# A graph attention layer with an MLP on one core: edges prepared on GpSimd, other places in the load queue, and a shorter last tile

## The reference

```python
xn = layernorm(x)                       # x: 1250 x 512, 20000 edges (src, dst)
q, k, v = xn@Wq + bq, xn@Wk + bk, xn@Wv + bv          # 4 heads of 512
alpha = sum(q[dst] * k[src]) / sqrt(512)              # one per edge and head
attn  = softmax of alpha over the edges of one dst
x_attn = segment_sum(attn * v[src], dst) + xn@Wskip + bskip
h = x_attn@Wlin + blin + x_attn[:, :512]
x = x + (gamma * (h - mean) / sqrt(var + 1e-5) + beta)
# second part, on z = layernorm(x): four groups of 16 columns are decoded to
# numbers, three MLPs (and, or, xor; 160 wide) run on rows 0 and 1, and of each
# only output column 64 is needed: relu(f@w1 + b1) @ w2[:, 64] + b2[64]
# the MLP is chosen by flags z[1:4]; its rounded output, clipped to 0..15, adds
# 2.0 to one of 16 columns of z (columns 80..95 and 96..111)
x = x + result
```

## Time and profile before

| | us |
|---|---|
| median of 3 runs | 1005.67 |
| lowest and highest of the runs | 1003.58, 1234.95 |
| the profiled execution's own time | 1004.65 |
| span of its instructions | 1002.5 |
| TensorE busy in the span | 984.4 |
| VectorE, ScalarE, GpSimd busy | 579.2, 335.0, 107.7 |

### The profile page before, as it was taken

The page is one execution under the profiler, slowest core; times in us unless marked ns, Lnnn a source line. Parts: engine busy times, 40 slices in busy tenths (PEclk is TensorE's granted clock), DMA queues, the critical chain, the costliest instruction groups (busy, mean ns, idle before and its releaser), DMA issues.

```text
span 1002.5 us, 13135 instructions
## 1 busy us (share of the span) xinstructions
PE 984.4 (98%) x4841; PEld 804.8 (80%) x4841; DVE 579.2 (58%) x1225; ACT 335.0 (33%) x531; POOL 107.7 (11%) x232
## 2 busy tenths in 40 slices
PE   9999999999999999999999999999999999999994
PEld 6667777688888888888888888888888888888883
DVE  6899996452445446226454542354464325788786
ACT  4446554102233223114222321233232213435342
POOL 2121101000000000000000000000000000345465
PEclk9999999999999999999999999999999999999997
DMA  9856554400152344005323420161334103443421
GB/s 327 286 210 210 218 192 189 168 2 1 53 189 68 91 122 146 28 1 157 111 79 105 159 83 1 27 215 53 105 80 163 52 1 83 154 121 105 143 83 40
DMA packets 43561, 115.84 MB, mean 116 GB/s; under 512 B 5472, under 2 KB 26044, under 8 KB 40172
## 3 DMA queue, kind: packets, MB, share of 16 engines
q1 hardware_dynamic: 38892, 98.21, 31.5%
q0 software_dynamic: 4608, 16.78, 4.3%
HBM read 70.07 MB, written 44.90 MB: 115 GB/s over the span
## 4 chain that ended last, share of the span: by engine, by line
PE 94%; DVE 2%; DMA 2%; ACT 1%; issue 1%; SPq 0%; DVEq 0%
PE ps_o L1533 10%; PE ps_o L1534 9%; PE ps_o L1535 9%; PE ps_s L1534 9%; PE ps_r L1533 9%; PE ps_s L1535 9%; PE ps_s L1533 9%; PE ps_r L1535 9%; PE ps_r L1534 9%; PE ps_t L1533 2%; PE ps_t L1535 2%; PE ps_t L1534 2%; DMA stage<-in_Wk 1%; PE ps_s L1612 1%; PE ps_s L1652 1%; DMA early<-in_Wlin 1%
## 5 line engine op out<-in xcount | busy, mean ns | idle before, releaser
L1534 PE MATMUL ps_s<-xT_lo,tT 128*128 128x512 f32 (+1 forms) x480 | 168.7, 351 | 0.0
L1535 PE MATMUL ps_s<-xT_hi,tT 128*128 128x512 f32 (+1 forms) x480 | 168.4, 351 | 0.0
L1533 PE MATMUL ps_s<-xT_hi,tT 128*128 128x512 f32 (+1 forms) x480 | 168.1, 350 | 0.0
L1533 PE MATMUL ps_o<-y,pT 128*128 128x512 f32 x380 | 148.6, 391 | 0.0
L1534 PE MATMUL ps_o<-y,pT 128*128 128x512 f32 x380 | 148.0, 389 | 0.0
L1535 PE MATMUL ps_o<-y,pT 128*128 128x512 f32 x380 | 148.0, 389 | 0.0
L897 ACT ACTIVATE prob<-prob,nbias 128x1250 f32<-128x1250 f32 x40 | 53.7, 1342 | 269.5 <-DVE nbias L1296 269.5
L1290 DVE CUSTOM_DVE_ANT_0 prob<-ps_s,maskb 128x1250 f32<-128x1250 f32 x40 | 58.2, 1456 | 128.9 <-issue 128.9
L1534 PEld LDWEIGHTS ps_s<-xT_lo,tT 128*128 128x128 f32 x480 | 90.7, 189 | 14.1
L1533 PEld LDWEIGHTS ps_s<-xT_hi,tT 128*128 128x128 f32 x480 | 90.5, 189 | 14.0
L1535 PEld LDWEIGHTS ps_s<-xT_hi,tT 128*128 128x128 f32 x480 | 90.8, 189 | 12.5
(11 more groups left out here) (293 smaller groups left out, 1763.0 us busy)
## 6 DMA issues: line engine op xcount, KB each, us to landing
regrouped<-prob SPq DMA_DIRECT2D x156, 160.0 KB, 2.8
whole<-regrouped SPq DMA_DIRECT2D x39, 640.0 KB, 3.9
products<-prod_parts POOLq DMA_DIRECT2D x32, 512.0 KB, 3.9
gbuf<-products SPq DMA_DIRECT2D x4, 2048.0 KB, 8.2
mbuf<-products SPq DMA_DIRECT2D x4, 2048.0 KB, 9.0
stage<-in_Wskip SPq DMA_DIRECT2D x4, 1024.0 KB, 6.0
stage<-in_Wq SPq DMA_DIRECT2D x3, 1024.0 KB, 5.5
stage<-in_Wk SPq DMA_DIRECT2D x3, 1024.0 KB, 5.9
```

Source lines behind the costliest of these rows:

```text
L1533: nc.tensor.matmul(out_, a[0], b[0], start=start, stop=False)
L1534: nc.tensor.matmul(out_, a[0], b[1], start=False, stop=False)
L1535: return nc.tensor.matmul(out_, a[1], b[0], start=False, stop=stop)
```

## The change

- `edge_places` moves from VectorE to GpSimd, where it becomes seven instructions ahead of all product stores. VectorE waits on `edges_ready` where it made them. The edges' four DMAs are issued ahead of operand 2.
- The six later tiles of x are issued behind operand 6, without the waits on stored products, and have a semaphore of their own (`x_more_in`), which VectorE waits for at tile 4.
- The first half of operand 2 is subtracted ahead of the save of block (0, 0), the second half behind it as before.
- `HID` goes from 160 to 162: the second bias of each MLP is the weight of one more hidden unit whose value is always 1. GpSimd's two bias instructions (L693, L694) and the bias DMA go.
- At the end `residual(NT - 1)` runs between the low columns and the decoding of tile NT-2, and the result columns of tile NT-2 are stored by ScalarE's queue.

```diff
-HID = 160
+HID = 162
@@ sync
-            for n in (3, 2):
-                sp.dma_start(early[n - 2][:], weights[n][0]).then_inc(early_in[n - 2], 16)
+            sp.dma_start(early[1][:], weights[3][0]).then_inc(early_in[1], 16)
             for i, ends in enumerate((src, dst)):
                 for a, w in EDGE_ROWS:
                     sp.dma_start(edge_i[a:a + w, i, :], ends[a:a + w, :]).then_inc(edges_in, 16)
+            sp.dma_start(early[0][:], weights[2][0]).then_inc(early_in[0], 16)
...
-            for i in range(KC - 1):
-                sp.wait_ge(prod_out[i], 16)
-            sp.dma_start(acc[:, X_ASIDE:NT - 1, :], x_tiles[:, X_ASIDE:NT - 1, :]).then_inc(x_in, 16)
-            sp.wait_ge(pads_ready, 1)
-            sp.dma_start(acc[0:LAST_ROWS, NT - 1, :], x[full:N, :]).then_inc(x_in, 16)
             for n in load_order():
                 sp.wait_ge(split_ready[n % 2], n // 2 - 1)
                 sp.dma_start(stage[n % 2][:], weights[n % 5][n // 5]).then_inc(stage_in[n % 2], 16)
+                if n == 6:
+                    sp.dma_start(acc[:, X_ASIDE:NT - 1, :], x_tiles[:, X_ASIDE:NT - 1, :]).then_inc(x_more_in, 16)
+                    sp.wait_ge(pads_ready, 1)
+                    sp.dma_start(acc[0:LAST_ROWS, NT - 1, :], x[full:N, :]).then_inc(x_more_in, 16)
...
-            for t in (NT - 1, NT - 2):
-                store_result(t)
+            sp.wait_ge(o_ready, NT - 1)
+            sp.dma_start(out[full:N, result_cols], acc[0:LAST_ROWS, NT - 1, result_cols]).then_inc(out_done, 16)
@@ gpsimd
+            def edge_places():
+                pool.wait_ge(edges_in, 32 * len(EDGE_ROWS))
+                link(nc.gpsimd.tensor_copy(edge_f[0:ER], edge_i[0:ER]))
+                source, place = edge_f[0:ER, 0, :], at_plane[0:ER, :]
+                link(nc.gpsimd.tensor_scalar(place, source, -float(NP // 2), 1.0 / NP, ALU.add, ALU.mult))
+                link(nc.gpsimd.tensor_scalar(place, place, ROUND, None, ALU.add))
+                link(nc.gpsimd.tensor_scalar(place, place, ROUND, None, ALU.subtract))
+                nc.gpsimd.tensor_scalar(weight_i[0:ER, :], place, DIGIT * 2.0 ** 23, ONE_BITS, ALU.mult, ALU.add)
+                link(nc.gpsimd.tensor_scalar(place, place, -float(NP), None, ALU.mult))
+                nc.gpsimd.tensor_tensor(edge_place[0:ER, :], place, source, ALU.add).then_inc(edges_ready, 1)
+            edge_places()
...
-                link(nc.gpsimd.tensor_scalar(sel_, sel_, s_b2[t % 2], 0.0, ALU.add, ALU.max))
-                link(nc.gpsimd.tensor_scalar(sel_, sel_, 15.0, ROUND, ALU.min, ALU.add))
+                link(nc.gpsimd.tensor_scalar(sel_, sel_, 0.0, 15.0, ALU.max, ALU.min))
+                link(nc.gpsimd.tensor_scalar(sel_, sel_, ROUND, None, ALU.add))
...
             z_factors(NT - 2)
             h_factor(NT - 1)
             choice(NT - 2)
-            chosen_bias(NT - 2)
             z_factors(NT - 1)
             choice(NT - 1)
-            chosen_gate(NT - 2)
+            gates(NT - 2)
             gates(NT - 1)
             results(NT - 2)
@@ scalar, at the end
                 feat_copy(NT - 1)
+                act.wait_ge(o_pool, 1)
+                act.dma_start(out[R * BY_POOL:R * BY_POOL + R, result_cols],
+                              acc[0:R, BY_POOL, result_cols]).then_inc(out_done, 16)
@@ vector
-            split_lo_halves(3)
+            split_lo_half(3, 0)
+            split_lo_half(3, 1)
+            split_lo_half(2, 0)
...
                 if p == 0:
                     if i == 0:
-                        split_lo_halves(2)
+                        split_lo_half(2, 1)
                     if i == 2:
-                        edge_places()
+                        dve.wait_ge(edges_ready, 1)
...
-                    dve.wait_ge(x_in, 48)
+                    dve.wait_ge(x_in, 16)
+                if t == X_ASIDE:
+                    dve.wait_ge(x_more_in, 32)
...
                 centre(NT - 1)
+                low_columns(NT - 2)
+                residual(NT - 1)
                 features(NT - 2)
-                residual(NT - 1)
                 choose(NT - 2)
```

More of the change, by code:

```diff
@@ L329, in graph_layer @@
         s_gate = [small[0:R, 78 + i:79 + i] for i in range(2)]
-        s_b2 = [small[0:R, 80 + i:81 + i] for i in range(2)]
         s_act, s_flag = [small[0:R, 82:83], flag_pool[0:R, 0:1]], [small[0:R, 83:86], flag_pool[0:R, 1:4]]
-        s_part = small[0:R, 86:89]
         s_sel, hot = [small[0:R, 90 + 2 * i:92 + 2 * i] for i in range(2)], small[0:R, 96:128]
-        x_in, edges_in, bias_in, tail_in = sem("x_in"), sem("edges_in"), sem("bias_in"), sem("tail_in")
-        blin_in = sem("blin_in")
+        x_in, edges_in, edges_ready, bias_in, tail_in = sem("x_in"), sem("edges_in"), sem("edges_ready"), sem("bias_in"), sem("tail_in")
+        blin_in, x_more_in = sem("blin_in"), sem("x_more_in")
         g_in, m_in, xres_in, out_done = sem("g_in"), sem("m_in"), [sem(f"xres_in{i}") for i in range(3)], sem("out_done")
@@ L559, in store_rest @@
                     sp.dma_start(out[R * t:R * t + rows, a:b], acc[0:rows, t, a:b]).then_inc(out_done, 16)
[L561 to L568, removed]
             def store(t):
@@ L1013, in split_lo, with split_lo_half @@
                                                 ALU.subtract).then_inc(split_ready[odd], 1)
-            def split_lo_halves(n):
-                for half, high in enumerate((half_hi[n - 2], hi_ready[n % 2])):
-                    some = half_cols(half)
-                    dve.wait_ge(high, 1)
-                    ins = nc.vector.tensor_tensor(opnd[n][1][:, :, some], raw(n)[:, :, some],
-                                                  opnd[n][0][:, :, some].bitcast(F32), ALU.subtract)
-                    if half:
-                        ins.then_inc(split_ready[n % 2], 1)
-                    elif n == 2:
-                        ins.then_inc(half_split, 1)
+            def split_lo_half(n, half):
+                some = half_cols(half)
+                dve.wait_ge(hi_ready[n % 2] if half else half_hi[n - 2], 1)
+                ins = nc.vector.tensor_tensor(opnd[n][1][:, :, some], raw(n)[:, :, some],
+                                              opnd[n][0][:, :, some].bitcast(F32), ALU.subtract)
+                if half:
+                    ins.then_inc(split_ready[n % 2], 1)
+                elif n == 2:
+                    ins.then_inc(half_split, 1)
             def onehots(b):
@@ L1422, in chosen_features @@
             def chosen_features(t):
+                low_columns(t)
                 features(t)
@@ L1439, in results @@
                 dve.wait_ge(gate_ready, t + 1)
-                chain(nc.vector.tensor_scalar(sel_, sel_, s_b2[t % 2], 0.0, ALU.add, ALU.max))
-                chain(nc.vector.tensor_scalar(sel_, sel_, 15.0, ROUND, ALU.min, ALU.add))
+                chain(nc.vector.tensor_scalar(sel_, sel_, 0.0, 15.0, ALU.max, ALU.min))
+                chain(nc.vector.tensor_scalar(sel_, sel_, ROUND, None, ALU.add))
                 for r in range(2):
@@ L1894 @@
         for r in range(2):
-            feats[:, o, r:4:2, r, o, :] = np.stack([w1[o][i] for i in (0, 1)])
-            feats[:, o, 4 + 3 * r:7 + 3 * r, r, o, :] = np.stack([w1[o][i] for i in (46, 44, 45)])
-            feats[:, o, 10 + r, r, o, :] = b1[o]
+            feats[:, o, r:4:2, r, o, 0:HID - 2] = np.stack([w1[o][i] for i in (0, 1)])
+            feats[:, o, 4 + 3 * r:7 + 3 * r, r, o, 0:HID - 2] = np.stack([w1[o][i] for i in (46, 44, 45)])
+            feats[:, o, 10 + r, r, o, 0:HID - 2] = b1[o]
+            feats[:, o, 10 + r, r, o, HID - 2] = 1.0
     arrays = {
@@ L1912 @@
         "mlp_w1": feats.reshape(FEAT_ROWS, 2, OPS * HID),
-        "mlp_w2": np.concatenate([g(f"L0_ffn_{o}_w2")[:, 64] for o in ops]),
-        "mlp_b2": np.stack([g(f"L0_ffn_{o}_b2")[64] for o in ops]),
+        "mlp_w2": np.concatenate([np.append(g(f"L0_ffn_{o}_w2")[:, 64], np.array([g(f"L0_ffn_{o}_b2")[64], 0], np.float32)) for o in ops]),
     }
```

36 lines of the change are left out of this document (10 added, 26 removed).

## The result

The changed kernel runs in 998.62 us (median of 6, 997.65 to 1000.16), the kernel before beside it in 1004.23 (median of 6): ratio 0.9946, 95% interval 0.9933 to 0.996. That is 5.6 us faster where 3.4 were forecast; by the 2% measure it is no change. One execution of the kernel before, at 1234.95 us, stands far apart from the others and is left out of the ratio. The profiled execution took 998.57 us, its span 996.4: 6.1 less than before.

A forecast was written before the change was run, and what follows sets the result against it. TensorE, busy 984.4 of 1002.5 us, bounds the kernel; only its idle time can be won. First place 0.7, second 1.6 and tail 1.1 sum to 3.4: 1004.65 - 3.4 = 1001.2 us, range 998.6 to 1004.8.

The forecast's parts named there:

- third and fourth place: Slow edge-counting matmuls of TensorE near 80 and 96 us; the prediction took these stretches for clean and gave no term.
- First place: Edge-counting matmuls from 32.40 us, waiting for VectorE's one-hots: 0.7 us gained of a possible 2.5.
- So the first one-hot comes at 23.2 and not at 21.7: VectorE waits for GpSimd's edges at the first counting place: first one-hot 1.5 us earlier than before, not 3.
- Blocking: GpSimd's edge instructions held up beside VectorE's splits: from 14.2, with 4.0 us of own work, done by 23.2.
- Now it is issued at 23.2; with the median 3.9 us of such a store it lands at 27.1: Store of block (0, 0), behind the edges in GpSimd's queue: VectorE waits 0.8 us, so 1.5 shrink to 0.7.
- Second place: Counting matmuls near 50 us, late because operand 6 landed late; with x tiles behind it, 1.6 us gained.
- Behind 51.6 the view shows no further wait of TensorE until the tail: Claim that after the second counting place TensorE waits nowhere before the tail, so nothing more to win there.
- Tail: Steps after the last aggregation matmul: sooner residual 0.8, split final stores 0.37, less 0.04 for extra columns: 1.1 us.
- The 0.37 for the stores: Two final stores at the end issued from SyncE and ScalarE's idle queue instead of both on SyncE: 0.37 us less.
- The slower one: Rival: blocked GpSimd edge chain ready at 28.2 delays the first place, 4.6 us lost there; 1006.5 us, chance 0.15.
- The first place goes altogether: Rival: edges ready by 19, first store out as before; 1000.1 us, or 999.4 with all 2.5; chance 0.2.
- move to operand 7: Rival: operand 7, queued behind x, lands at 52 and holds VectorE; 1002.8 us; chance 0.2, shared with nothing at first place.

The follow-up runs named there:

- run 6: Changed kernel with GpSimd's first edge instruction, the copy, done nine times instead of once: 1004.05 us, ratio 1.0004.
- run 1: Changed kernel with the edges' places worked out on VectorE again and the edge DMAs behind operand 2: 999.44 us, ratio 0.9957.
- run 3: Changed kernel with both halves of operand 2 subtracted behind the save of block (0, 0) again: 998.94 us, ratio 0.9956.
- run 10: The changed kernel itself measured and profiled again, nothing edited: 999.14 us, ratio 0.9961.
- run 5: Changed kernel with the second bias added by GpSimd again, 160 units, the residual early as changed: 999.59 us, ratio 0.9965.
- run 7: Changed kernel with the first product's four stores issued by SyncE instead of GpSimd's queue: 998.06 us, ratio 0.9949.
- run 2: Changed kernel with the six later x tiles ahead of operand 6 again, with their waits on stored products: 1000.15 us, ratio 0.9965.
- run 12: Changed kernel with GpSimd's first edge instruction, the copy, done three times: 999.34 us, ratio 0.9958.
- run 4: Changed kernel with the last residual behind the decoding of tile 8 again: 1000.21 us, ratio 0.9966.
- run 9: Changed kernel with edges on VectorE and both halves of operand 2 together again, leaving the x tiles and tail edits: 1001.2 us, ratio 0.9974.

## Why the prediction was right and where it was not

The range holds, 998.62 within 998.6 to 1004.8, and no change by 2%. That it holds is luck: three of the six runs lie below 998.6, and the gain was 5.6 where 3.4 were forecast. The mechanisms were right, the terms were sized too small, and the third and fourth place were missed.

**First place, predicted 0.7, measured 2.07.** Two steps failed. The first is "So the first one-hot comes at 23.2 and not at 21.7". It came at 23.13, but that it agrees is chance: Wlin was 1.3 us later than in the kernel before (VectorE's first instruction on it 14.51 against 13.22, by which the prediction worked); from there the one-hots are 2.84 earlier than before, near the 3.0 of VectorE alone, and they waited for no edge. GpSimd's own work, taken at 4.0 us, was right: run 6, where VectorE leaves it alone from 23.5 on, shows six instructions from 23.51 to 26.97 and a copy near 0.45. Blocking was taken at 5.0 us (14.2 to 23.2 less 4.0) and was 3.0 (15.38 to 22.40 less 4.0), since GpSimd gets one instruction through per split. The second is "Now it is issued at 23.2; with the median 3.9 us of such a store it lands at 27.1", and with it 0.8 us of waiting at block (1, 0). The store was issued at 22.34, since the edges were ready sooner, and let ScalarE go at 26.35, 4.0 us later; VectorE, there at 26.94 (forecast 26.9), saved at 27.05. So the median fitted this store, and the issue was wrong. But it is no law: with issues at 19.8 (before), 20.3 (run 1), 20.8 (run 3), 21.6 (run 10), 22.0 (run 5) and 22.3 (after) ScalarE went on at 26.03, 26.05, 26.04, 25.57, 25.78 and 26.35, so an earlier issue did not bring an earlier landing, as run 7 shows too. In runs 2, 12 and 4, with issues at 21.8, 22.3 and 22.4, it was 26.76, 26.84 and 28.03, and VectorE waited 1.09, 0.64 and 1.75 us: the wait that the prediction saw is real in some executions. What holds the landing back is likely the loads in flight (the DMA share is 0.92 over the first 25 us before); no run isolates them. Together VectorE's stretch from Wlin to the end of the batch is 2.65 shorter (22.31 to 19.66), where 0.7 was forecast. TensorE takes 2.07 of it, and the rest is chance at the start: against TensorE's first matmul Wlin came 0.42 later than before, and TensorE reached the counting 0.16 sooner. In run 10 it takes 2.54 (3.28 to 0.74).

**Second place, predicted 1.6, measured 1.78.** Operand 6 was rounded from 37.88 on without a wait, an us sooner than the forecast 39 to 41. But the cause that the prediction names is only half of it: with the x tiles back (run 2) TensorE loses 0.20 there, with only the x tiles moved (run 9) it loses nothing but, by the reckoning there, the clock's part. Either edit removes this wait; the gains of the two are not a sum.

**Third and fourth place, not predicted, 0.86 and 0.58.** The failed sentence is "Behind 51.6 the view shows no further wait of TensorE until the tail". It was read from the matmuls' row of that view, 2.7 us in 2 waits; the row of their weight loads, 7.3 us in 22, was left aside. The earlier trace rows were one link of the chain near 80 and served only as a sample of blocking. The x tiles behind operand 6, for which the prediction had only the 1.6 near 50, are paid mostly here: run 2 gives back all of the third place, and run 9, with the x tiles alone, keeps it.

**Tail, predicted 1.1, measured 1.62.** The residual starts 0.03 behind its power, as forecast; run 4 prices it at 0.96 where 0.8 of 0.97 were taken. GpSimd was free for L661 only because the bias went: 1.23 by run 5. The prediction named this as a condition and gave it no term. The 0.37 for the stores and the 0.04 for the six columns were not isolated.

**Start, predicted nothing, measured -0.87.** Chance, by run 10.

So 0.7 + 1.6 + 1.1 against 2.07 + 1.78 + 1.62, and 1.44 for the places not seen; 0.81 for the start and the rest go off.

**The rivals.** The slower one, GpSimd's edge chain as the new bound, did not come: the edges came at 22.40, far from its 28.2. Run 6 made it happen, and its mechanism holds, its price roughly: edges at 26.97 bring the kernel to 1004.05, level with before, where the prediction put the point of no gain "later than about 26". "The first place goes altogether" (1000.1 or 999.4) was nearest: the first store let ScalarE go only 0.3 later than before with Wlin 1.3 later, though the edges were not ready by 19. The stall did not move to operand 7: no wait of TensorE near 59.

The Trainium skill, "SBUF — State Buffer", section "Who interferes with whom", has a VectorE instruction with two SBUF inputs contend with a GpSimd instruction that reads SBUF, and the later one blocked until the first is done. The runs show contention on both sides: the edge chain takes 3.0 us more than its free durations, and three VectorE splits take 3.74 us beside it against 3.50 in run 1, where GpSimd stands idle. By the rule taken literally for a row of splits back to back, as the prediction did, the four last edge instructions would have begun after 21; three of the four had begun by 19.27. The measurement decides.

## What to carry to other kernels

Before writing "no further wait", read the rows of the weight loads beside those of the matmuls, or the view of each line that could wait: a short matmul that is a few tenths late shows no gap of its own, and such waits were worth over a third of what the two large ones were. Before pricing a transfer by its issue plus the median of its group, move its issue in a run: here an earlier issue brought no earlier landing, and the same issue landed up to 1.7 us apart. When two edits ease the same wait, undo each alone: here either was nearly enough at one place, and at the tail undoing either cost most of the gain. Profile the same kernel twice before giving a stretch a price below 0.5 us.

## What was not expected of the hardware

- A 512 KB store of GpSimd's, issued from 19.8 to 22.4 us, let its buffer go at 25.6 to 26.4 in seven of ten profiles, whatever its issue; in runs 2, 12 and 4 it was 26.76, 26.84 and 28.03 for issues at 21.8, 22.3 and 22.4. Issued at 26.92 (run 6) it was 30.29.
- Beside back-to-back VectorE splits GpSimd's instructions of 0.33 to 0.64 us took 0.87 to 1.56 us, about one for each split of 1.2 us, and the splits slowed as well: 1.17 us each in run 1, 1.25 in the kernel after, up to 1.47 in run 6.
- An idle time of 1.45 us of TensorE (run 9) and one of 2.82 (run 6) were followed by a stretch partly at 1.2 GHz (granted clock 0.57 from 37 to 41 us, 0.72 from 36 to 42); one of 1.74 in the profiled execution of the kernel before was not. Of the 48 runs of the kernel before beside the experiments 22 have a mean granted clock of 0.992 or less (3 of 14, 9 of 17, 10 of 17), of the 12 of the changed one none; whether it is such a stretch in those runs, no profile shows. What it costs there is open: a TensorE that is later also waits less near 50 us.
